# A graph network with a routed MoE layer on one core: new order of routing and a longer lead, with a group's scatter and its add of z ahead of the last tile's store

## What is computed

```python
x = x + gnn(layernorm(x), edges, edge_type, ...)      # two layers: segment sums of gated edge messages, plus x @ root + bias
t = layernorm(x)
probs = softmax(t @ gate_w.T + gate_b)                # 8 experts
top_v, top_i = top_k(probs, 2)                        # two of them kept, with their probabilities as weights
shared = sum over 2 shared experts of gelu(t @ sw1.T + sb1) @ sw2.T + sb2
routed = sum over the 2 kept experts of weight * (gelu(t @ rw1.T + rb1) @ rw2.T + rb2)
x = x + shared + routed
```

## Time and profile before

| | |
|---|---|
| median of 3 runs | 1766.83 us (1765.28 to 1771.9) |
| the profiled execution | 1758.73 us |
| its span, first to last instruction | 1757.0 us |
| PE, DVE, ACT, POOL busy | 87%, 55%, 41%, 37% of the span |
| PE's granted clock over the span | 0.953 of full |

### The profile page before, as it was taken

How to read it: one execution, slowest core, us unless ns; L and a number is a source line. 1 busy time by engine, 2 the same in 40 slices (tenths; PEclk the granted TensorE clock), 3 DMA queues, 4 the chain that set the end, 5 groups by cost and what they waited for, 6 DMA issues and landing times. The chain is left out here.

```text
span 1757.0 us, 27836 instructions
## 1 busy us (share of the span) xinstructions
PE 1523.2 (87%) x8640; PEld 1216.1 (69%) x8640; DVE 963.2 (55%) x2837; ACT 711.8 (41%) x1232; POOL 655.9 (37%) x988
## 2 busy tenths in 40 slices
PE   7999999889979999999996736788788778878997
PEld 5777667777856777788875525676676667767886
DVE  5555777767523333466643565566465556645553
ACT  3334345556511112256652433454354345432331
POOL 3752142567530000026653344344334434432222
PEclk9999999999999999999998868999899999999999
DMA  9999997977689999967768855555545545432220
GB/s 245 272 282 306 281 308 231 292 133 121 95 200 288 280 278 278 300 187 124 136 105 185 204 162 163 162 159 155 181 132 173 175 148 156 132 103 98 100 75 17
DMA packets 115238, 325.96 MB, mean 186 GB/s; under 512 B 17244, under 2 KB 17770, under 8 KB 109859
## 3 DMA queue, kind: packets, MB, share of 16 engines
q1 hardware_dynamic: 77202, 211.19, 40.5%
q0 software_dynamic: 37904, 113.12, 28.0%
HBM read 205.63 MB, written 121.74 MB: 186 GB/s over the span
## 5 line engine op out<-in xcount | busy, mean ns | idle before, releaser
L1192 ACT ACTIVATE th<-bank 128x512 fp32r<-128x512 f32 x158 | 94.1, 596 | 284.8 <-PE bank L1467 284.6
L1120 POOL DMA_INDIRECT out<-xt,out_row x90 | 91.9, 1021 | 187.9 <-DVE xt L2169 169.6
L1812 DVE SCALAR_TENSOR_TENSOR tl<-bank,th 128x512 fp32r<-128x512 f32 x79 | 54.5, 690 | 190.9 <-ACT th L1192 190.8
L1447 PE MATMUL bank<-root2h,th 128*128 128x512 f32 x316 | 134.5, 425 | 18.3 <-DVE tl L1812 15.6
L984 POOL DMA_INDIRECT gx<-y,dst_slot x42 | 45.4, 1082 | 266.5 <-ACT xn_e L1212 242.6
L1447 PE MATMUL bank<-root1h,th 128*128 128x512 f32 x316 | 133.2, 422 | 7.2 <-DVE yout L1841 4.5
L1447 PE MATMUL bank<-root2l,th 128*128 128x512 f32 x316 | 127.2, 402 | 0.0
L1447 PE MATMUL bank<-root1l,th 128*128 128x512 f32 x316 | 126.5, 400 | 0.0
L1447 PE MATMUL bank<-root2h,tl 128*128 128x512 f32 x316 | 126.2, 400 | 0.0
L1447 PE MATMUL bank<-root1h,tl 128*128 128x512 f32 x316 | 125.6, 397 | 0.0
L1614 PE MATMUL bank<-ident,xt 128*128 128x128 f32 x360 | 57.7, 313 | 77.1 <-DMA xt<-sorted_rows 77.1
(11 more groups left out here) (292 smaller groups left out, 4490.3 us busy)
## 6 DMA issues: line engine op xcount, KB each, us to landing
basis_t<-in_gnn_basis SPq DMA_DIRECT2D x64, 896.0 KB
xt<-sorted_rows SPq DMA_DIRECT2D x45, 560.0 KB, 4.0
xin<-in_x SPq DMA_DIRECT2D x39, 512.0 KB, 8.7
xin<-y SPq DMA_DIRECT2D x39, 512.0 KB, 8.1
zr<-in_x SPq DMA_DIRECT2D x19, 1024.0 KB, 5.2
zr<-z POOLq DMA_DIRECT2D x19, 1024.0 KB, 8.1
y<-yout SPq DMA_DIRECT2D x37, 512.0 KB, 8.9
z<-yout SPq DMA_DIRECT2D x34, 512.0 KB, 7.7
```

The source lines that it names most:

```text
L1120: pool.indirect_dma_start(out=out, in_=xt[i % 4][:, j, 0:H], in_offset=None, out_offset=bass.IndirectOffsetOnAxis(ap=out_row[:, i % 4, j:j ...
L1192: act.activation(th_a[:, s, :], tpb[s][:], f).then_inc(s_hi, 1)
L1447: ins = pe.matmul(out_ap, a(k), b(k), start=first, stop=last)
L1812: ins = dve.scalar_tensor_tensor(out=tl_a[:, s, :], in0=tpb[s][:], scalar=0.0, in1=th_a[:, s, :].bitcast(F32), op0=ALU.max, op1=ALU.subtract)
```

## The change

- Lead: a group is ranked and scattered in an even slot, one slot earlier than before with respect to the tiles that need it, and right after the weighting in that slot; it is turned in an even slot and routed in an odd slot ahead of that. SP loads tile i+3 in slot i instead of i+2, and x of a group earlier.
- Buffers: x and z of a group go straight into `stage` (now four buffers, rows of 560 numbers of which 512 are x's), normalised in place; `zr` is gone.
- Order on every engine within a slot, and of `TURNS`; PE turns the hidden tile before the next tile's parts, and reads the next pick ahead of the last product.
- GpSimd in an even slot: extras, the scatter of the group, the add of z, then the store of the last tile.
- Routing arithmetic: the bias is added by ACT at the evacuation; the two kept experts are found on the logits and exp is taken of both sets; ranks are counted from a running limit instead of `seen`; a pick takes two DVE instructions less.
- Ahead of the slots: nine late steps come first, four z adds are issued together, and groups 0 to 4 are taken through with a new interleaving.

```diff
@@ buffers and slots @@
-        zr, z1 = place("zr", [P, 2, QT, H], at=q1)
+        stage0q, z1 = place("stage0q", [P, QT, XW], at=q1)
...
+        stage = (stage0q, stage1q, stage2q, stage3q)
...
         def turned_in_slot(i):
+            return group_at(i, 10)
+        def routed_in_slot(i):
             return group_at(i, 9)
-        def routed_in_slot(i):
+        def ranked_in_slot(i):
             q = (i + 8) // 2
-            return q if i % 2 == 0 and LEAD_GROUPS - 1 <= q < NQ else None
...
+            return q if i % 2 == 0 and q < NQ else None
@@ SP @@
             def load_group(q):
-                wait(sp, s_qn, QT * (q - 1))
-                sp.dma_start(zr[:, q % 2, 0:tiles_of(q), :], q_rows(x, q)).then_inc(s_zin[q % 2], 16)
+                wait(sp, s_sorted[q % 4], 16 * QT * (q // 4))
+                sp.dma_start(stage[q % 4][:, 0:tiles_of(q), 0:H], q_rows(x, q)).then_inc(s_zin[q % 4], 16)
...
             for i in range(NF):
-                if exists(i + 2):
-                    load_tile(i + 2)
+                if exists(i + 3):
+                    load_tile(i + 3)
@@ GpSimd @@
+            for q in range(4):
+                sort_rows(q)
+                if q:
+                    add_z(q + 3)
             group_rstd(4)
             group_extras(4)
...
             for i in range(NF):
                 q = ranked_in_slot(i)
-                if q is not None and q > 4:
-                    group_extras(q)
+                if q is not None:
+                    if q > 4:
+                        group_extras(q)
+                    sort_rows(q)
+                if group_at(i, 14) is not None and group_at(i, 14) > 6:
+                    add_z(group_at(i, 14))
                 if i:
                     store_tile(i - 1)
                 if exists(i + 1):
                     rows_of_tile(i + 1)
-                if group_at(i, 13) is not None and group_at(i, 13) > 6:
-                    add_z(group_at(i, 13))
-                if q is not None:
-                    sort_rows(q)
-                if group_at(i, 10) is not None and group_at(i, 10) > 5:
-                    group_rstd(group_at(i, 10))
+                if group_at(i, 11) is not None and group_at(i, 11) > 5:
+                    group_rstd(group_at(i, 11))
@@ TensorE @@
+            for e in range(LAST_E - 1):
                 late2_step(e)
             pe.wait_ge(s_msg, 2 * ET)
             turn_group(0)
+            late2_step(LAST_E - 1)
@@ VectorE, in a slot @@
                 for c in range(2):
                     weigh(i, c, chunks[c])
+                if q_rank is not None:
+                    positions(q_rank)
                 shared_lo(i)
+                routed_lo(i)
                 if exists(i + 1):
                     f_lo(i + 1, "a")
                     f_lo(i + 1, "b")
-                routed_lo(i)
-                if q_rank is not None:
-                    positions(q_rank)
+                if q_route is not None:
+                    route_a(q_route)
                 for t in picked_in_slot(i):
                     pick_tile(t)
                 if q_first is not None and q_first > 5:
-                    q_stats(q_first, range(1))
+                    q_stats(q_first, range(2))
...
                 if q_route is not None:
-                    route_a(q_route)
                     route_b(q_route)
+                    sort_kinds(q_route)
```

More of the change, by code:

```diff
@@ L419, in gnn_moe_kernel @@
         s_token = sem("tokens_written")
-        s_sorted = [sem(f"rows_sorted{i}") for i in range(3)]
+        s_sorted = [sem(f"rows_sorted{i}") for i in range(4)]
         s_pick = sem("tile_picked")
@@ L823, in load_tile @@
                 sp.wait_ge(s_pick, i + 1)
-                for k in range(3):
-                    wait(sp, s_sorted[k], 16 * sum(tiles_of(n) for n in range(k, q + 1, 3)))
+                for k in range(4):
+                    wait(sp, s_sorted[k], 16 * sum(tiles_of(n) for n in range(k, q + 1, 4)))
                 if i < 4:
@@ L835, in _ @@
             load_group(0)
+            load_group(1)
             load_up_experts()
-            load_group(1)
-            for g in range(NG - 1, NG + 1):
+            for g in range(NC // 2 + 4, NG + 1):
                 sp.wait_ge(s_tp, Step(SE, Pos(2 * (g - 4) + 1)).T.k + 1)
                 load_pair(SE, Pos(g))
-            for q in range(2, 6):
-                load_group(q)
+                if g < NG:
+                    load_group(2)
+                else:
+                    load_group(3)
+            load_group(4)
+            load_group(5)
             sp.wait_ge(s_pads, 16 * 2 * NKIND)
@@ L1315, in q_norm @@
                 act.wait_ge(s_qst, q + 1)
-                wait(act, s_sorted[q % 3], 16 * QT * (q // 3))
-                wait(act, s_qtp, KC * (q - 1))
                 for j in range(tiles_of(q)):
-                    act.activation(stage[:, q % 3, j, 0:H], zr[:, q % 2, j, :], ACT.Identity, bias=qnmr[:, s, j:j + 1],
+                    rows = stage[q % 4][:, j, 0:H]
+                    act.activation(rows, rows, ACT.Identity, bias=qnmr[:, s, j:j + 1],
                                    scale=qrstd[:, s, j:j + 1]).then_inc(s_qn, 1)
@@ L1409, in _ @@
             f_shares(0)
+            for k in range(KC):
+                q_full(4, k)
+            q_logits(4)
+            q_exp(4)
             q_norm(5)
@@ L1678, in turn_group @@
                     q_transpose(q, k)
-            for e in range(6):
+            for e in range(LAST_E - 1):
                 late2_step(e)
@@ L1735, in _ @@
                     q_transpose(q_turn, 3)
-                if q_route is not None:
-                    logits_by_token(q_route)
-                for j in range(2):
-                    down_routed(i, j, chunks)
+                down_routed(i, 0, chunks)
+                if exists(i + 1):
+                    turn_tile(i + 1, "x")
+                    chosen = picked(i + 1)
+                down_routed(i, 1, chunks)
         @block.vector
@@ L2077, in route_b @@
                 for j in range(n):
[L2078 removed]
+                    ins = dve.match_replace(lg[:, 1, j, :], topv[:, j, :], lg[:, 0, j, :], -1.0e30)
                 link(ins)
[L2080 to L2082 removed]
@@ L2206, in _ @@
             pick_tile(2)
+            q_stats(4, range(QT))
+            for part in ("a", "b"):
+                f_lo(0, part)
+            route_a(4)
             q_stats(5, range(QT))
+            route_b(4)
+            sort_kinds(4)
             for i in range(NF):
-                q_route, q_rank, q_first, q_more = routed_in_slot(i), ranked_in_slot(i), group_at(i, 11), group_at(i, 10)
+                q_route, q_rank, q_first, q_more = routed_in_slot(i), ranked_in_slot(i), group_at(i, 12), group_at(i, 11)
                 if i:
```

438 lines of the change are left out of this document (198 added, 240 removed).

## The result

The changed kernel takes **1659.03 us** (median of 4 runs, 1654.61 to 1662.86) against 1767.23 us of the kernel before on the same chip: ratio 0.938, 95% interval 0.935 to 0.941. The forecast was 1659 us.

The account below looks back on a forecast made before the run. Bound in the routing slots by a five-engine loop longer than PE's work, with PE waiting for tile loads. Span 1757.0 - 112 (slots) + 4 (up to slot 2) = 1649, 1651 for that execution, plus 8.1 for the median: 1659 us; range 1632 to 1704.

Parts of the forecast that it names:

- What bounds it, and that the gap goes: Routing slots: a loop through five engines makes PE wait for the tile load; the change removes that wait.
- So a pair is 25.5 + 0.6 = 26.1 us.: Pair of slots with a group: 25.5 us of PE work plus 0.6 us standing still for DVE's weighting.
- The cover of the late store: Last tile's store, behind the z add, delays tile i+3's load: 1.3 us to spare, 0.5 us a pair added.
- Slots 2 to 32: 406.: Slots 2 to 32: 406 us instead of 518.2, a gain of 112 us.
- Up to slot 2: +4.: From 930 us to slot 2: it starts at 1099.5 against 1095.29, 4 us later; bounds -10 and +15.
- The last twelve slots stay.: Last twelve slots: no change, since the loads of picks on PE's sequencer lie under queued matmuls.
- The median.: Whole kernel: the median of the runs lies 8.1 us above the profiled execution, 1659 instead of 1651 us.
- No pressure from the add of z: Rival, GpSimd's z add in the slots: takes 8.1 us, cover 4.7 us, kernel 1638 us; chance 0.12.
- The late store: Rival, GpSimd's queue: stores land 4.3 us later, every pair waits 3 us, 1701 us; chance 0.17.
- Slower, by the same place: Rival, GpSimd's stores behind the scatter: pairs wait 10 us, 1799 us, slower than before; chance 0.03.
- The gap stays: Rival: SP's tile load stays released by the group's last scatter, PE still waits, 1767 us; chance 0.03.
- A longer table switch: Rival, ACT in the slots: two table switches of a pair take 1.4 us longer each, 1698 us; chance 0.03.

Follow-up runs that it names:

- register loads early: Changed kernel with VectorE's two register loads of a tile's chunk numbers made one slot earlier: 1644.0 us, 0.933 of the kernel before.
- loads early and lead-in: Also "the version with everything": changed kernel, register loads a slot early, group 4's rstd before group 6's z add, first late pairs' adds behind two z adds: 1617.7 us.
- probe: Changed kernel with some 10 more register loads a slot on VectorE, values unused, a measurement and not a candidate: 1722 us.

## Why the prediction was right, and where not

- *What bounds it, and that the gap goes.* Right, and shown: no PE wait on a tile load in slots 2 to 32, clock 1.00, and the gap is back when the scatter comes a pair later. Of my other signs the gelu's end held (T+5.5, with the start of slot 10 as T) and about the store's landing (by T+23 for 25); the pair of 26 to 26.7 us and the add's 11 us did not, and one sign of being wrong came true: VectorE is not ready when the gelu is done.
- *"So a pair is 25.5 + 0.6 = 26.1 us."* Pairs are 27.25 in the mean of 14 (1101.86 to 1483.39, slot 30's marker). The 0.6 of the even slot came as 0.31. The step that failed is "Odd slot: logits fill the time of the gelu, no stop": I looked only at ScalarE's side. VectorE does two picks, four statistics, two `f_out` and two register loads ahead of the weighting, and the register loads, which I did not cost, take 3 us there. With them off the path a pair is 25.9. The rows could have told me: in the kernel before the gelu ended at 1352.50 and the weighting began at 1353.90, behind 1.22 us that are put down to issue; they are two register loads of 0.30 us and what goes with them. The late evacuations no row of before could show: there the evacuation starts 0.04 us behind PE in every slot from 2 to 30.
- *The cover of the late store, "1.3 us, too thin to cost at nothing: I add 0.5 us a pair."* Mis-sized. Slot 10 begins at 1210.5. I had z through at T+24.5, the stores landed at T+27 and the load at T+31.6. SP issues the load at 1234.17, T+23.7, and the median landing of such a load is 4.1 us later, T+27.8; PE turns that tile in slot 12, at 1245.4, T+34.9. The cover is 7 us. The term behind it is the add of z: issued at 1223.56, it and both stores were through by 1234.17, within 10.6 us, so 11.5 us for the add alone was too much, and my lower bound of 8.1 was nearer. The trace of "register loads early" has the landings themselves: 8.6 us in the median of the 16 adds behind 1000 us, 7.7 to 13.8. Between the late pair's landings (23.9 us behind four adds of z, 15.1 behind two, from the issue of the late add at 958.52 to VectorE's start at 982.37, and from 958.42 to 973.55 in the version with everything) an add takes 4.4 us of the queue.
- *"Its issue on GpSimd stays at 1.0."* 1.35 to 1.38 us. Hidden.
- *Slots 2 to 32: 406.* 415.0. Of the 9 us too little, +19 is what went with the edit to the register loads (by the traces 9 of it in the odd slots, where they stand in the way, and 10 in the even slots with the late evacuations), the cover that was not needed is -7, and the pair without both -3 (25.9 against 26.1).
- *Up to slot 2: +4.* +3.6 from the first add of z, +1.5 from where that lies. The size was right and a term was not: the late pair landed at 982, not 994, since adds of z in 2 KB pieces go faster one behind another than I had them. GpSimd's wait for group 6's rows (8.88 us) and the clock (0.50 in 1000 to 1050) came as forecast.
- *"The last twelve slots stay."* 1.4 us less (140.6 behind slot 33's marker against 142.05).
- *The median.* +8.1 us not found, as told above. The hit is two errors of 8 us with opposite signs.
- *Rivals.* No pressure from the add of z: right in its mechanism, a cover that is wide, but its 1638 us were not reached because of the register loads and the late evacuations. The late store does not bind; no pair shows it. Slower, by the same place: the mechanism is real at a lead of one pair less (1869 us), and the change has one slot to spare. The gap stays: no. A longer table switch: no; ScalarE's loads still start 0.02 us after the work before and the next step 0.01 us after them. The drain of the Trainium skill (ScalarE: Activation LUTs, What ACT_TABLE_LOAD costs) is not in this trace, with two switches 3 us apart either.

## What to carry to other kernels

When a loop through several engines is opened by more lead, the lead makes the gain; test the order in the queues apart from it, since an order that no longer guards anything can still cost (13 us of 415 here). Count an engine's register loads as work with a place of their own, and do them a step early, in a wait that is there anyway: here that took 19 us of 415 away. Then look where in the loop the gain lies before you name its cause: only 9 of the 19 lay behind the loads that were moved. And rest no thin cover on a DMA price from a lone transfer: four adds one behind another took 4.4 us each.

## What I had not expected of the hardware

A register load from SBUF on VectorE took 0.30 us in 60 of 60 cases that lay 11 us or more behind the issue of an add of z and 3.8 us or more behind that of a store, and 0.4 to 1.8 us from 1 us behind the issue of the add to some 5 us behind it, with the stores issued in between. In about the same stretch of GpSimd's queue a signal of PE came late: at ScalarE by 1.4 to 1.5 us in 11 even slots of after, and, without the add, at VectorE, which stood still for 2.5 us, 12 times. With the same order and distance in GpSimd's queue "register loads early" has no late evacuation and "loads early and lead-in" four, so that stretch alone does not bring them. VectorE's small steps ran beside the scatters at their usual 0.15 to 0.27 us. The Trainium skill (SBUF — State Buffer, SBUF: two separate sides) tells of a lock between VectorE and GpSimd that holds for whole instructions. It may have a part here, but what it tells is of instructions that use those ports, and neither a register load nor a signal from PE to ScalarE is one that it names; no run here tells these apart, and which path is congested stays open. That the same code reaches its first add of z anywhere from 949.9 us (probe) to 968.3 us stays open too; no experiment went ahead of 930 us.
